# A scatter pair waits for the pair before it, in a fused attention and mixture-of-experts kernel

## The reference

```python
x = x + xattn(layernorm(x), ctx, ctx, mask, ...)       # 8 batches, 16 heads
xf = layernorm(x).reshape(-1, 256)                       # 4096 tokens
ys = geglu(xf @ Ws1 + bs1) @ Ws2 + bs2                   # shared network
logits = (xf @ Wr + br) / 1.5
top_val, top_idx = top_k(logits, 2)
top_w = softmax(top_val)                                 # two of twelve experts
yE = geglu(xf @ We1[e] + be1[e]) @ We2[e] + be2[e]       # for the chosen e
x = x + ys + sum_k top_w[k] * yE[top_idx[k]]
```

## Time and profile before

| | |
|---|---|
| median of the timed runs | 1086.86 us |
| lowest to highest of 3 | 1084.34 to 1089.44 us |
| span of the profiled execution, first to last instruction | 1085.2 us |
| PE busy | 957.5 us (88%) |
| DVE busy | 714.1 us (66%) |
| ACT busy | 569.3 us (52%) |
| POOL busy | 373.7 us (34%) |

### The profile page before, as it was taken

The page is one execution under the profiler, slowest core; times in us unless marked ns, Lnnn a source line. Parts: engine busy times, 40 slices in busy tenths (PEclk is TensorE's granted clock), DMA queues, the critical chain, the costliest instruction groups (busy, mean ns, idle before and its releaser), DMA issues.

```text
span 1085.2 us, 26548 instructions
## 1 busy us (share of the span) xinstructions
PE 957.5 (88%) x7515; PEld 696.9 (64%) x7515; DVE 714.1 (66%) x1842; ACT 569.3 (52%) x1276; POOL 373.7 (34%) x537
## 2 busy tenths in 40 slices
PE   5588899989888887979399889999989999999996
PEld 4233445535354344758188778888768888898885
DVE  5776778878676735646078557776636677667753
ACT  3136565655545565323054457667535667657653
POOL 5300212344443453132700044445323345335342
PEclk9779999999999999989589989999999999999999
DMA  4552315263362142144463473545324355435332
GB/s 152 132 105 81 95 55 137 90 149 86 104 157 62 41 144 74 60 148 150 153 221 117 140 216 52 140 123 144 48 33 128 49 139 138 94 85 138 48 54 42
DMA packets 107927, 117.34 MB, mean 108 GB/s; under 512 B 20396, under 2 KB 99960, under 8 KB 107648
## 3 DMA queue, kind: packets, MB, share of 16 engines
q1 hardware_dynamic: 87168, 67.97, 23.4%
q0 software_dynamic: 20064, 47.20, 17.6%
q10 hardware_dynamic: 560, 0.53, 0.1%
HBM read 73.91 MB, written 38.87 MB: 104 GB/s over the span
## 4 chain that ended last, share of the span: by engine, by line
PE 40%; issue 5%; DMA 3%; DVE 3%; another core or an unknown queue 2%; ACT 1%; DVEq 1%; SPq 0%; ACTq 0%; POOL 0%; POOLq 0%
PE ff_psH L2300 24%; PE ff_psY L2327 13%; PE ff_psX L2254 2%; DVE ff_actf L2553 1%; PE ff_psH L2269 1%; DMA out_dram<-ff_x 1%; DMA ff_xrow<-expert_in 1%; DMA expert_in<-ff_zeros 1%; PE ff_psY L2284 1%; DVE ff_actl L2546 1%; DMA ff_x<-out_dram 1%; ACT ff_gel L2394 0%; DVE ff_ysb L2629 0%; DVE ff_x L2570 0%
## 5 line engine op out<-in xcount | busy, mean ns | idle before, releaser
L2300 PE MATMUL ff_psH<-xh,ff_wx 128*128 128x256 f16 (+1 forms) x1776 | 271.0, 264 | 15.1 <-issue 9.7
L1126 DVE TENSOR_REDUCE fast_negm<-fast_psS 128x2 f32<-128x512 f32 x256 | 168.5, 686 | 85.0 <-PE fast_psS L514 75.4
L2300 PE MATMUL ff_psH<-xl,ff_wx 128*128 128x256 f16 (+1 forms) x888 | 218.7, 264 | 0.0
L886 ACT ACTIVATE fast_PT<-fast_psT 128x512 f32<-128x512 f32 x256 | 147.3, 596 | 119.9 <-PE fast_psT L546 102.2
L2235 POOL DMA_INDIRECT out_dram<-ff_ysc,ff_trow x78 | 125.6, 1610 | 194.0 <-ACT ff_ysc L2442 175.4
L2300 PEld LDWEIGHTS ff_psH<-xh,ff_wx 128*128 128x128 f16 x1776 | 167.5, 99 | 37.2 <-issue 13.9
L2553 DVE SCALAR_TENSOR_TENSOR ff_actf<-ff_psH,ff_b1T,ff_gel 128x256 f32<-128x256 f32 (+1 forms) x234 | 106.0, 454 | 101.4 <-ACT ff_gel L2394 99.7
L2394 ACT ACTIVATE ff_gel<-ff_psH,ff_b1T 128x256 f32<-128x256 f32 (+1 forms) x234 | 105.4, 451 | 82.5 <-PE ff_psH L2300 62.8
L514 PE MATMUL fast_psS<-fast_Kz,fast_Qs 128*128 128x512 f16 x256 | 101.8, 403 | 35.1 <-DVE fast_negm L1126 25.0
L2327 PE MATMUL ff_psY<-ff_wx,ff_acth 128*128 128x256 f16 x792 | 132.2, 273 | 0.6 <-DVE ff_actl L2546 0.5
L2389 ACT ACTIVATE ff_acth<-ff_actf 128x256 f16<-128x256 f32 (+1 forms) x282 | 110.5, 392 | 33.3 <-DVE ff_actf L2553 31.3
(11 more groups left out here) (276 smaller groups left out, 1672.6 us busy)
## 6 DMA issues: line engine op xcount, KB each, us to landing
ff_st<-in_L_ffn_We_dram POOLq DMA_DIRECT2D x12, 1536.0 KB
ff_xrow<-expert_in SPq DMA_DIRECT2D x41, 256.0 KB
ff_st<-in_L_ffn_We_dram POOLq DMA_DIRECT2D x12, 768.0 KB
fast_Qs<-qstk SPq DMA_DIRECT2D x48, 128.0 KB
fast_xbuf<-in_x_dram SPq DMA_DIRECT2D x8, 512.0 KB, 5.1
fast_words<-in_mask_BxSxS_bk_dram SPq DMA_DIRECT2D x8, 512.0 KB, 3.7
fast_xres<-in_x_dram SPq DMA_DIRECT2D x8, 512.0 KB, 4.1
out_dram<-fast_x1s SPq DMA_DIRECT2D x8, 512.0 KB, 5.1
```

The lines of the kernel that those rows point to most:

```text
L886: nc.scalar.activation(PT[:, n % NPT, :], psT[n % 2][:], ACT.Exp).then_inc(sem["exp_done"], 1)
L1126: nc.vector.tensor_reduce(negm[:, two(b), t, 2 * p:2 * p + 2], src, AX.X, ALU.max, negate=True).then_inc(sem["max_done"], 1)
L2300: mm = nc.tensor.matmul(psH[j % stage.banks][:, (half + 1) * NB - rows:(half + 1) * NB], a[:, dt, lo:lo + P], x[:, dt, NB - rows:], start= ...
```

## The change

Both scatter loops get a wait. From the second tile on POOL waits, before it issues the two scatters of a tile, until the semaphore that all scatters of this batch (or of this loop) count up has reached 32 for each tile issued, which is when both scatters of the tile before have landed. In `place_value` the value read is also masked with 64*64*32-1, which changes no value.

```diff
         def scatter(b):
             until(pool, "place_link", of("place_link", b, 5), alone=True)
             for t in range(QT):
+                if t >= 1:
+                    until(pool, "scattered", of("scattered", b, 32 * t), alone=True)
                 for k in range(2):
                     pool.indirect_dma_start(out=scratch["xs"][:, :],
...
     def place_value(eng, e):
-        return nc.values_load(place_i[0:1, bass.ds(e, 1)], engines=[eng.engine], min_val=0, max_val=(NBLK * PLACE + PLACE) * OVER - 1,
+        value = nc.values_load(place_i[0:1, bass.ds(e, 1)], engines=[eng.engine], min_val=0, max_val=(NBLK * PLACE + PLACE) * OVER - 1,
                                skip_runtime_bounds_check_because="built on chip from counts whose sum is two rows a token")
+        return value & (PLACE * PLACE * OVER - 1)
...
         for t in range(LEFT * QT):
+            if t >= 1:
+                pool.wait_ge(scattered, 32 * t)
             for k in range(2):
                 pool.indirect_dma_start(out=xs[:, :], in_=keep["xn2"][:, NT - LEFT * QT + t, :], in_offset=None,
```

## The result

The changed kernel took 1079.06 us (median of 6 runs, 1075.66 to 1080.87) against 1087.53 us for the kernel before in the same measurement (1084.34 to 1091.61): a ratio of 0.993, interval 0.990 to 0.995. That is 8 us faster; the forecast was 17. The profiled execution has a span of 1079.3 us (before 1085.2) and a granted clock of 0.961 (0.954).

The account below looks back on a forecast made before the run. PE bounds the kernel (88% busy), losing 26.2 us beside feed_forward's scatters. Terms -23.4+2.0+3.4+0.8 = -17.2 us against the 1085.2 span give 1068.0, with 1.7 for timed runs 1070 us; range 1054 to 1090 (8 in 10).

Parts of the forecast that it names:

- Feed_forward, -23.4: In feed_forward, spacing the 24 scatters recovers most of the 26.2 us PE loses beside them: -23.4 us.
- A wait costs 2.8 us: On POOL, each new wait for a pair's landing adds 2.8 us, bounds 1.2 and 4.45.
- Attention, +3.4: In the attention stage, three waits per batch over five batches cost +3.4 us in sum, from -9.7 to +20.5.
- my own formula: Attention: delay is the batch's lengthening (8.4 us) less POOL's earlier idle time and, in the first three batches, 1.2 us slack.
- The first batch: Attention's first eight scatters: 8.4-5.5-1.2 = +1.7 us, DVE waiting for POOL in place of the stall.
- The last three batches: Attention: third batch covered and 2.5 us won, fourth covered at 0, fifth +3.5 us.
- The weight load, +2.0 (0 to 3.9): In feed_forward, POOL's weight load moves beside running blocks and slows the store of x1; half of 3.9 us counted.
- The mask, +0.8: One more register operation per expert on each engine, 0.063 us twelve times: at most +0.8 us on PE.
- The signs: Expected traces: feed_forward copies under 11 us apart; ln2 released by POOL in three or more slots; slot 5 shorter.
- rival C: Slow landing beside attention's loads, 4.45 us a wait: +5.9 us, 1093 us; chance 0.06.
- A: Rival: spacing relieves nothing, the loss hangs on the number of scatters: +8.7 us, 1095.6 us; chance 0.13.
- B: Rival: pairs fill nearly half of POOL's time, so half the stall stays: -5.6 us, 1081 us; chance 0.12.

Follow-up runs that it names:

- e2: Waits only in the attention stage, mask kept, none in feed_forward, against the kernel before: 1099.0 us, ratio 1.012.
- e1: Waits only in feed_forward, mask kept, none in the attention stage, against the kernel before: 1065.2 us, ratio 0.982.
- e3: Only the mask, no wait in either loop, against the kernel before, on the chip with the stall: 1087.5 us, ratio 1.0015.
- f1: Only the mask, no waits, against the kernel before, on a chip without the stall: 1050.5 us, ratio 1.003.
- f2: The changed kernel again, against the kernel before, on a chip without the stall: 1077.3 us, ratio 1.0295.
- e8: Waits in feed_forward; in attention none, the eight scatters cut by POOL's other work into four and two pairs; against the kernel before: 1056.9 us, ratio 0.9725.
- g3: Attention scatters spread between POOL's other work without waits, feed_forward waiting before every second pair, against the kernel before, chip without the stall: ratio 1.000.
- k2: Repeat in another group: attention scatters spread without waits, feed_forward in rows of four, against the kernel before, no stall: ratio 0.999.
- f4: No waits; ten tiny POOL operations between feed_forward's pairs, against the kernel before, chip without the stall, repeated in a later group: ratio 1.005.
- e6: No waits; ten tiny POOL operations between feed_forward's pairs, against the kernel before, chip without the stall: 1053.3 us, ratio 1.005.
- e7: Waits only in feed_forward, second expert's weight load issued ahead of the 24 scatters, against the kernel before, chip without the stall: 1051.2 us, ratio 1.002.

## Why the prediction was wrong in size

**The range and the sign held, the gain was half of the forecast.** By its steps:

- *Feed_forward, -23.4.* Right. 25.8 us came back; e2 shows that they belong to this loop alone. The reading "PE starves beside a row of scatters" was right for the chip of the trace, though of the 13 matmuls between 522 and 532 us only 7 have the gap, not each. ACT's copies stand under 11 us apart, PE waits by "issue" once, for 0.4 us, and the last scatter was issued at 578.0, inside 553 to 588.
- *A wait costs 2.8 us.* As a mean right (2.7 over all 26), in its distribution wrong. In `feed_forward` the idle times are 2.3 to 2.9 us, 2.0 to 2.6 net of the 0.3 of before. In attention they are 3.97, 5.36, 3.16 in the first batch, 4.67, 4.98, 4.49 in the second, 4.48, 2.29, 2.29 in the third, and 2.27 to 2.29 in the last two. The 15 average 3.0 us net, but those of the first two batches, where the cover is thin, cost 3.9 and 4.4. In the trace of before the transfer engines were 79, 82 and 89% busy during the first three batches and 26 and 27% during the last two. In the changed kernel they are 45 to 79% busy during attention's seven waits of 3.2 to 5.4 us, and 16 to 41% during the four of 2.3 us in the third batch and the start of the fourth. But in `feed_forward` they are 60% busy on average and no wait is over 2.9 us, so the busy share alone doesn't set the landing; what else does isn't shown. The row that I used as a lower bound came from a quiet stretch.
- *Attention, +3.4.* This is the step that failed: it measured +14.0 (against before; 9 to 14 against the three traces, before, e1 and e3, in which this stage has no waits). The miss is slot 5. Slots 3 and 4 together cost 1.0 us (forecast +1.7), slot 6 gave 0.5 back (forecast 0), and the part behind it cost 4.6 (forecast 3.5). Slot 5 was to become 1.8 us shorter (+0.7 of delay, -2.5 of relief) and became 9.3 longer. Two things are in it. The first is the size of the wait: POOL's second batch took 13.2 us more, not 8.4. The second is that I took each batch by itself. Behind a late slot POOL comes late to the next batch: the second one began 17.7 us before the end of slot 4, and now 12.1. With these 5.6 us my own formula gives 13.2+5.6-6.5-1.2 = 11.1 us of delay for `ln2`, and reckoned from the start of slot 5 it stood 10.8 later (12.7 us in, before 1.8). Slot 5's own stall gave some of it back, and +9.3 came.
- *The first batch* came out near by two errors that cancel. POOL was at it for 21.8 us in place of 10.5, so the formula gives 11.3-5.5-1.2 = +4.6, and reckoned from the start of slot 3 `ln2` was 5.0 later. But the stall's relief, which I had struck out for slots 3 and 4, came all the same: slot 3 was 3.9 us shorter, and as much came back in slot 4 behind `ln2`.
- *The last three batches.* The third batch's cover was enough, as forecast, and the fourth cost nothing. For the fifth the 4.6 against 3.5 proves little: its batch grew by 6.3 us, not 8.4, and the stretch behind slot 6 took 97.5, 98.3 and 104.4 us in the three traces without waits there (102.1 in the changed kernel).
- *Relief and cover are the same microseconds.* Slot 3 did win its 3.9 us, and this shortened the time that POOL had for the first batch. f1, without the stall, has only 2.4 us where I counted on 5.5. I had written that DVE would wait for POOL in place of the stall, and then took the idle times from a trace with the stall all the same.
- *The weight load, +2.0 (0 to 3.9).* The mechanism was the one named, the store beside the load takes 5.64 us, but the cost was 3.6, near the upper end. Half was chosen on the ground that a block leaves SP slack; what had none was the queue behind the store on SP: the zero rows, the first expert rows, then PE. In e1 it cost 6.2.
- *The mask, +0.8.* Between 0 and 5 us; not resolved.
- *The signs.* `ln2` had POOL's step as its releaser four times, as forecast; but slot 5 became longer, not shorter, and slots 3 and 4 took 44.3 and 54.7 us, not 48 to 50. POOL's waits over 4 us were my sign of rival C, and five of the fifteen in attention are.
- *The rivals.* A was refuted on the chip with the stall: 25.8 us came back. Beside rows, two rules of the Trainium skill spoke for it: transfer engines go round their queues packet by packet ("DMA: Bandwidth & Descriptors", section on queues, rings and completion order), and instruction fetch is "mostly hidden" ("Runtime: NRT & Kernel Launch", section on instruction fetch mechanics). The four chips without the stall agree with them. Whether the chip with the stall contradicts them isn't shown, since its gaps need not be waits for a fetch (see the lines below). C was the nearest to what happened in the first two batches, 3.9 and 4.4 us a wait, about where I had put the end of the gain. But it held for those alone, not for all 26 waits. Of B, half relief, nothing came: the stall in `feed_forward` went almost whole.

**What the forecast could not see** is that the stall isn't a property of the kernel alone. On the one other chip where the same change ran (f2) it makes the kernel 3% slower: no stall to remove, and 28.6 us more in attention.

What makes the stall on one chip stays open. It needs a row of scatters (e1, e8), the load on the transfer engines alone doesn't make it (they move less in the trace with the stall), and POOL issues at the same rate in both. Nor do the rows show a fetch behind each gap: between 508.3 and 539.4 us of the trace of before PE has 12 gaps by "issue", while two packets went over the instruction queues (waits of PE; the view of the transfers, with packets, MB and share):

```profile
PE ff_psH L2300 <- issue: 12.1, 12, 2.4
```

```profile
q8 instruction: 1, 0.02, 0.2%
q14 instruction: 1, 0.01, 0.1%
```

Whether the unbroken issuing or the number under way counts was asked five times with two in flight, never on a chip with the stall.

## What to carry to other kernels

A wait added to an engine that others depend on costs the whole delay less the idle time that will be there once the change has acted, not the idle time in the trace of before; follow the lateness from one slot into the next, and price each wait by the traffic beside it. To break up a row of issues, place other work of the same engine between them rather than a wait, as e8 did: with the stall this won 12.4 us in the attention stage against e1, and without it it cost nothing (g3, k2). Before paying for the removal of a stall that the profile ascribes to nothing, measure the kernel on a second chip.

## What the runs showed of the hardware that I had not expected

- The same program runs 36 us (3.4%) apart on different chips: 1084 us on one, 1047 to 1050 on four others, with equal times in the experts. Between e3 and f1 the difference lies in the two stages in which POOL sends rows of eight and 24 scatters.
- A pair of scatters lands in 2.3 us (POOL's idle time from the end of the second issue to the next start) where the transfer engines are 16% busy, and in up to 5.4 us where they are 79% busy with the attention stage's transfers, but in 2.3 to 2.9 us in `feed_forward`, at 60% on average; this is alike on both sorts of chip (2.28 and 2.8 to 5.3 us in f2).
- A 1.6 MB write of zero rows issued 1.3 us behind the start of a 2.3 MB weight load lets the next step of SP follow 16.8 us later (f4, and e6 alike); issued 12 us behind the load, 8.7 us later (the changed kernel), which is no more than with the load long over (9.1 us in e7).
